# Last stage of a cross-attention and fast-feedforward kernel: two batches' score products ahead of the first probabilities, the first transposes ahead of the FFN's last output product

## What is computed

```python
def _fff(x, node_w, node_b, w1, b1, w2, b2):
    # a token walks 4 levels of a tree and ends in one of 16 leaves
    hidden_all = relu(einsum('nd,ldh->lnh', xf, w1) + b1)
    hidden = hidden_all * one_hot(leaf)
    return einsum('lnh,lho->no', hidden, w2) + one_hot(leaf) @ b2
...
q, k, v = _fff(x, q_...), _fff(x, k_...), _fff(x, v_...)
attn = softmax(einsum('bqd,bkd->bqk', q, k) / 16, axis=-1)
return einsum('bqk,bkd->bqd', attn, v)
...
x = x + _L0_xattn_ref(_layernorm(x), ctx, ctx, w_q, w_k, w_v, w_o)
x = x + _L0_ffn_ref(_layernorm(x), ...)
```

## Time and profile before

| | us |
|---|---|
| median of 3 executions | 640.76 (640.52 to 642.57) |
| the profiled execution | 640.1 |
| its span in the profile | 638.3 |
| PE busy in the span | 586.1 (92%) |
| DVE busy | 439.1 (69%) |
| ACT busy | 299.0 (47%) |
| POOL busy | 236.9 (37%) |
| last product of stage 2 ends, last stage begins | about 550.7 |

### The profile page before, as it was taken

How to read it: one execution, slowest core, us unless ns; L and a number is a source line. 1 busy time by engine, 2 the same in 40 slices (tenths; PEclk the granted TensorE clock), 3 DMA queues, 4 the chain that set the end, 5 groups by cost and what they waited for, 6 DMA issues and landing times.

```text
span 638.3 us, 14744 instructions
## 1 busy us (share of the span) xinstructions
PE 586.1 (92%) x5131; PEld 494.5 (77%) x5131; DVE 439.1 (69%) x1511; ACT 299.0 (47%) x482; POOL 236.9 (37%) x298
## 2 busy tenths in 40 slices
PE   8677999999899999999999897859999999799996
PEld 7566888877788887888888686848888888689995
DVE  2765666988788898898898787873555555156664
ACT  4104544544444453554445355007877787533331
POOL 6700010143143243334323326660006666666551
PEclk9869999999899999999999899879999999999999
DMA  6798788898998898899898749977999999766653
GB/s 190 221 305 261 237 230 226 252 260 238 283 271 249 286 310 247 258 297 283 251 296 275 208 134 303 309 254 274 324 364 387 411 408 375 258 191 197 200 177 126
DMA packets 99639, 169.58 MB, mean 266 GB/s; under 512 B 12848, under 2 KB 67824, under 8 KB 99568
## 3 DMA queue, kind: packets, MB, share of 16 engines
q1 hardware_dynamic: 87712, 141.83, 70.5%
q0 software_dynamic: 9216, 25.18, 12.5%
q10 hardware_dynamic: 2640, 1.65, 0.9%
HBM read 92.59 MB, written 75.50 MB: 263 GB/s over the span
## 4 chain that ended last, share of the span: by engine, by line
PE 51%; DMA 26%; SPq 13%; DVE 5%; issue 3%; ACT 1%; POOL 1%; DVEq 0%; ACTq 0%; POOLq 0%
DMA parts_dram<-k_lo 9%; DMA k<-parts_dram 8%; PE banks L840 6%; PE banks L825 6%; PE banks L814 6%; DMA parts_dram<-q_lo 5%; SPq L334 5%; PE banks L882 4%; PE banks L903 4%; PE banks L530 4%; PE banks L545 4%; PE banks L557 3%; SPq L317 2%; PE banks L871 2%; PE banks L573 2%
## 5 line engine op out<-in xcount | busy, mean ns | idle before, releaser
L1537 POOL DMA_INDIRECT xs_dram<-xn2s,place x96 | 95.7, 997 | 159.4 <-ACT pt L936 142.4
L1174 DVE TENSOR_REDUCE mneg<-banks 128x2 f32<-128x512 f32 x240 | 121.8, 548 | 44.9 <-PE banks L546 43.8
L936 ACT ACTIVATE pt<-banks 128x768 f32<-128x768 f32 x128 | 103.5, 810 | 102.2 <-PE banks L558 101.7
L545 PE MATMUL banks<-k,q 107*128 107x256 f32 x240 | 76.4, 369 | 17.7 <-DMA k<-parts_dram 10.9
L557 PE MATMUL banks<-q,k 109*128 109x256 f32 x256 | 74.0, 341 | 2.0 <-DMA q<-m_lo 0.3
L545 PEld LDWEIGHTS banks<-k,q 107*128 107x128 f32 x240 | 46.5, 194 | 29.3 <-DMA k<-parts_dram 16.3
L558 PE MATMUL banks<-q,k 109*128 109x128 f32 x256 | 57.3, 224 | 0.0
L573 PE MATMUL banks<-pt,vp 128*32 128x256 f32 (+1 forms) x1024 | 56.4, 339 | 0.4 <-ACT pt L936 0.4
L1596 POOL DMA_INDIRECT q_all<-ys_dram,place x32 | 30.8, 964 | 67.1 <-DMA ys_dram<-yb 53.8
L546 PE MATMUL banks<-k,q 107*128 107x128 f32 x240 | 54.4, 227 | 0.0
L557 PEld LDWEIGHTS banks<-q,k 109*128 109x128 f32 x256 | 48.7, 190 | 6.8 <-ACT pt L936 5.7
(11 more groups left out here) (177 smaller groups left out, 1290.9 us busy)
## 6 DMA issues: line engine op xcount, KB each, us to landing
ys_dram<-yb SPq DMA_DIRECT2D x36, 512.0 KB, 6.2
xb<-xs_dram SPq DMA_DIRECT2D x35, 512.0 KB, 7.7
k<-parts_dram SPq DMA_DIRECT2D x128, 128.0 KB, 3.8
q<-parts_dram SPq DMA_DIRECT2D x64, 256.0 KB, 4.6
xs_dram<-zero SPq DMA_DIRECT2D x45, 256.0 KB
xs_dram<-zero SPq DMA_DIRECT2D x18, 384.0 KB, 4.8
tables<-leafw SPq DMA_DIRECT2D x16, 257.0 KB, 8.2
xt<-x SPq DMA_DIRECT2D x16, 256.0 KB, 4.9
```

The lines of the kernel that those rows point to most:

```text
L545: mm(ps[:, 0:S], q[0:KN, t, P:S], k[0:KN, t, :], start=True, stop=True)
L936: nc.scalar.activation(pt[:, 2 * p:2 * p + 2, :], st_banks(b, p)[:, :, 0:S + P], ACT.Exp, scale=SC).then_inc(exp_sb, 1)
L1174: last = nc.vector.tensor_reduce(mneg[1 - u][:, t, 2 * j:2 * j + 2], S_BANKS[:, :, cols], axis=AX.X, op=ALU.max, negate=True)
L1537: gp.indirect_dma_start(xs_dram[tree], bass.IndirectOffsetOnAxis(ap=place[:, k:k + 1], axis=0), xn2s[m % RING][:, t, :], None).then_inc(sc ...
```

## The change

PE now does transposes(0) between block_out(34) and block_out(35). The wait for both y copies is split: quad 34's stands ahead of probs_T(0), quad 35's ahead of probs_T(1). scores(1) moves ahead of the first `finals`, and with it `copy_qT(1)` ahead of `exps(0)` on ACT, and `copy_kT(1)` ahead of `maxima(0)` and `maxima(1)` ahead of `copy_pT(0)` on DVE. On ACT `copy_qT(0)` moves ahead of `copy_y(35)`. On POOL the v rows of batch 0 come right behind the first 18 k rows; the two late k rows that stood ahead of them are put in later, one of them in the turn of batch 3 and one in that of batch 6. `KFIRST` falls from 5 to 3, so that transposes(0) waits for fewer k rows. From batch 2 on PE, ACT and DVE have the same order as before, and no instruction is added or taken away.

```diff
-KFIRST = 5
+KFIRST = 3
...
-            pe.wait_ge(y_sb, Q)
-
...
                     if u + 2 < U or more:
                         transposes(i + (u + 2) // U, (u + 2) % U)
+                    if i * U + u < 2:
+                        pe.wait_ge(y_sb, Q - 1 + i * U + u)
                     probs_T(i, u)
-                    if u + 1 < U or more:
+                    if (u + 1 < U or more) and i * U + u > 0:
                         scores(i + (u + 1) // U, (u + 1) % U)
...
-            transposes(0, 0)
+            block_T(0)
+            block_T(1)
+            block_h(0)
+            for q in range(Q):
+                if q + 2 < Q:
+                    block_T(q + 2)
+                if q + 1 < Q:
+                    block_h(q + 1)
+                if q == Q - 1:
+                    transposes(0, 0)
+                block_out(q)
             scores(0, 0)
             transposes(0, 1)
+            scores(0, 1)
             finals(0, True)
...
+                if q == Q - 1:
+                    copy_qT(0, 0)
                 copy_y(q)
...
-            copy_qT(0, 0)
+            copy_qT(0, 1)
             exps(0, 0)
-            copy_qT(0, 1)
             finals(0, True)
...
                         copy_kT(i + (u + 2) // U, (u + 2) % U)
+                    if i * U + u == 0:
+                        maxima(0, 1)
                     copy_pT(i, u)
-                    if u + 1 < U or more:
+                    if (u + 1 < U or more) and i * U + u > 0:
                         maxima(i + (u + 1) // U, (u + 1) % U)
...
             copy_kT(0, 0)
+            copy_kT(0, 1)
             maxima(0, 0)
-            copy_kT(0, 1)
             finals(0, True)
...
-            gp.wait_ge(tq_ps, 1)
-            late_row(0)
-            gp.wait_ge(s2_ps, 1)
-            late_row(1)
             for s in range(QB):
                 gp.wait_ge(y_out[s], 16 * TREES * QUADB // QB)
             for t in range(T):
                 v_row(0, t)
+            late = 0
             for b in range(NB - 1):
-                if b + 2 < (NB - KB) * T:
-                    gp.wait_ge(tq_ps, min(b + 3, NB))
-                    late_row(b + 2)
+                for _ in range(2 if b in (3, 6) else 1):
+                    if late < (NB - KB) * T:
+                        gp.wait_ge(tq_ps, min(b + 3, NB))
+                        late_row(late)
+                        late += 1
                 gp.wait_ge(pT_ps, b + 1)
```

More of the change, by code:

```diff
@@ L1046, in _, with copy_qT @@
             Q = TREES * QUADB
+            def copy_qT(i, u):
+                b = i * U + u
+                act.wait_ge(tq_ps, b + 1)
+                ge(act, s2_ps, b - 1)
+                nc.scalar.copy(qT[u % 2][:], banks[0][:]).then_inc(qT_sb, 1)
             copy_xT(0)
```

## The result

The changed kernel took 638.07 us as the median of 22 executions, the kernel before 642.06 in 22 taken with them (its first three had a median of 640.76). The ratio is 0.9936, with a 95% interval of 0.9913 to 0.996: 2.6 to 5.6 us less. Single executions scatter by several us in both (633.1 to 641.0 and 637.6 to 647.2).

What follows compares the result with a forecast made beforehand. PE bounds the stage in full flow, but 5.69 of the 18.09 us ahead of it are waits and fills. The steady order was to begin at 564.59 instead of 567.70: 640.76 - 3.1 = 637.7 us, range 636.6 to 639.6.

Steps and rivals of the forecast that it cites:

- Steps 1 to 3: PE from 549.61: transposes(0) 0.87 us, quad 35's output product 1.12, then scores(0) directly at 551.60 instead of 553.78.
- Scores(0): PE's first scores, right behind quad 35's output product, were to run from 551.60 to 553.33, 1.73 us.
- The fill of scores(1): Scores(1) on PE were given 1.73 us (555.07 to 556.80); only the low bound had them fill in 1.98.
- The low bound of the prediction: Scores(1) and probs_T(1) 0.23 us later each, scores(1) filling in 1.98 instead of 1.73: a gain of 2.4.
- The hand-overs: Start of PE's transposes to DVE's copy 0.91 us, to ACT's 0.47; if as from an idle PE, 0.23 later.
- Steps 5 and 9: PE idle 0.87 us ahead of scores(1) for DVE's k copy, and 1.5 ahead of probs_T(1).
- Step 6 and the rule of strict order: Maxima(0) stand behind DVE's copy of k(1); engines can't pass a waiting instruction, so 1.5 us of stall stay.
- v and x1r: v lands 2.6 us ahead of values(0), x1r costs 0.2 at most; rival of late v, 12 in 100, gain 1.6.
- Late k rows: Batch 3 has four gathers, 5.0 us in a turn of 4.77; batches 9 and 10 come 19 us later: free.
- fewer k rows first: Transposes(0) need the sixth k row, landed by 539.4 and wanted at 549.61: ten us of cover, no cost.
- The wait for y: Waits for y(34) and y(35), met at 550.7 and 552.7, ahead of probs_T(0) at 557.7 and probs_T(1) at 560.5: no cost.
- The clock: Rival: the granted clock falls in PE's new gaps of 0.9 and 1.5 us; 2 in 100.

Runs made afterwards that it cites:

- e8: Changed kernel with transposes(0) ahead of block_out(34) instead of block_out(35); last block_h to scores(0) took 4.44 us against 4.65.
- e5: Changed kernel with maxima(0) and maxima(1) on DVE ahead of the copies of k(1) and k(2); ratio 0.9992 against the kernel before.
- e6: Changed kernel with the two late k rows ahead of batch 0's v rows; scores(0) to transposes(4) took 14.07 us against 13.01.
- e7: Changed kernel with transposes(1) ahead of scores(0) on PE and maxima(1) ahead of the copy of k(2) on DVE; ratio 0.9975 against the kernel before.
- e10: The same kernel as e7, run again; ratio 0.9939 against the kernel before.
- e13: The unedited kernel before, traced on a chip with late signals; last block_h to transposes(4) took 24.22 us.
- e12: The unedited changed kernel on a chip with late signals; ratio 1.0036 against the kernel before.

## Why the prediction was right or wrong

- **Sign, size and range** held: 637.7 us was forecast, 638.07 measured, with 636.6 to 639.6 as the range. That they meet so closely is luck. The forecast was taken off 640.76, and with more executions the kernel before had 642.06, 1.3 more; the medians then differ by 4.0 instead of 3.1, 0.9 more. The two nearly cancel. By difference, 3.1 us was forecast, the timing says 2.6 to 5.6, the traces 2.4.
- **Steps 1 to 3**, transposes(0) ahead of the output product and scores(0) right behind it: right in order, 0.33 too early in the sum. Mis-sized terms: transposes 1.02 instead of 0.87 and the output product 1.30 instead of 1.12. I had taken both from places where groups of one shape follow each other. With each change of shape PE's weight loads pause 0.17 to 0.23 us (e8).
- **Scores(0)** took 1.92 of the chain instead of 1.73, the same cause. Together these are 0.52 of the missing 0.65 us. The fill of scores(1) adds 0.24 (1.97 in the chain instead of 1.73), and about 0.1 of it comes back behind the k copy of batch 2, which the maxima follow after 0.69 instead of 0.75. The low bound of the prediction, a gain of 2.4, is the number that came, but mostly not by its terms: of the three only this fill did. The hand-overs stayed at the forecast 0.91 from the start of the transposes to the k copy (550.98 to 551.89, 554.70 to 555.61), and the changes of shape took their place.
- **Steps 5 and 9**, the two waits: right in place and cause. Forecast 0.87 and 1.5 us, measured 0.88 and 1.29 between products.
- **Step 6 and the rule of strict order**: the stall did move from ACT to DVE, and cost 1.2 us (e5 without it), where I had put 1.5.
- **v and x1r**: no wait, as forecast; counted to the product of values(0) (560.65), as the forecast was, the cover is 2.4 us instead of 2.6. In e6, e7, e8 and e10 values(0) wait for v, by 0.25 to 1.19 us. The estimate of 3.2 us for the store was drawn from the Trainium skill, "DMA: Bandwidth & Descriptors" (section Anatomy of one DMA), whose fit is for a DMA that GpSimd issues; this store is issued by SP. Nothing in the sum goes by it. **Late k rows** and **fewer k rows first**: no wait of PE for them in the changed kernel's chain (its stretch behind transposes(4) is 70.9 against 70.98).
- **The wait for y** was put at nothing: right.
- **The clock**: I let it fall only in the new gaps, and in the changed kernel's first trace it stays at 1.00 there. Where signals are late it falls in both orders: in the old one's gap when the y copy is late (0.50, e13), where the changed one keeps 1.00, and in the changed one's behind transposes(4) (0.57, e12).
- **What I didn't foresee** is that the gain isn't there under all conditions: with late signals it was not measurable (1.0036). New waits stand behind transposes(4), with a lower clock after them in e12, and the table has them in every run of the experiments that holds both parts. Why they come only there stays open.

## What to carry to other kernels

At the seam of two stages, lay the new order out instruction by instruction from the marks of the trace, and put the fills and pauses between groups in as terms: here they were a fifth of the forecast gain. When a wait is moved, look at the idle time ahead of the instruction that now blocks: DVE stood idle 2.2 and 3.4 us ahead of its copies, the last 0.9 of each with ready maxima behind them, and turning the two around made that stretch another 1.2 us shorter, though the gain wasn't seen in the whole time. A gain read from one place in a trace should be looked for behind that place too, and on a second chip.

## What the runs showed of the hardware

- PE's weight loads pause 0.17 to 0.23 us where the shape of products changes, and not at a semaphore wait that is already met (e8). What causes it stays open.
- On the four chips of the experiments the same kernel took 663 to 668 us instead of 642, at a mean granted clock of 0.94 to 0.96 against 0.965, with PE's signals seen 1 to 5 us late, often by two or three engines at once. The cause stays open.
- After idle times of 2.82 and 0.88 us the granted clock was 0.50, and eight records of 256 columns took 3.75 us instead of 1.98 (e13). After one of 2.09 it was 0.57 (e12); after one of 2.22 in e5 it stayed at 1.00.
